# Two-layer gated cross-attention block: another way to turn the attention probabilities of layer 1

## What is computed

```python
def _L1_xattn_ref(X, encoder_out, Wq, bq, Wkv, bkv, Wo, bo):
    Q = (X @ Wq.T + bq).reshape(b, lq, h, d)
    KV = (encoder_out @ Wkv.T + bkv).reshape(b, lk, h, 2 * d)
    K, V = (KV[..., :d], KV[..., d:])
    scores = jnp.einsum('bqhd,bkhd->bhqk', Q, K) / SCALE
    weights = jax.nn.softmax(scores, axis=-1)
    attn = jnp.einsum('bhqk,bkhd->bqhd', weights, V).reshape(b, lq, h * d)
    return attn @ Wo.T + bo
```

## Time and profile before

| | us |
|---|---|
| median of 3 runs | 1371.87 (1369.77 to 1372.11) |
| the profiled execution, its own time | 1371.72 |
| its span in the profile | 1370.0 |
| PE, DVE, ACT, Pool busy | 1223.5, 1026.2, 769.0, 395.0 |
| mean granted clock of PE | 0.972 of 2.4 GHz |

### The profile page before, as it was taken

One profiled execution on the slowest core, in us unless ns is written; L12 is line 12 of the kernel. 1 busy time (PEld: TensorE's weight loads), 2 busy tenths in 40 slices (PEclk: granted clock), 3 DMA queues, 4 the chain that ended last, 5 costly groups with the idle time before them and its releaser, 6 DMA issues.

```text
span 1370.0 us, 27816 instructions
## 1 busy us (share of the span) xinstructions
PE 1223.5 (89%) x10408; PEld 760.9 (56%) x10408; DVE 1026.2 (75%) x1662; ACT 769.0 (56%) x1013; POOL 395.0 (29%) x248
## 2 busy tenths in 40 slices
PE   0869899999999996788799999999999999999974
PEld 0335565566566566334356666656666666666642
DVE  6656666666666646877888888888888888888877
ACT  0525455555555555455666666666666666666642
POOL 6357666666566415332000000000000000000000
PEclk9979999999999997999999999999999999999996
DMA  5223244234333420010011110011110011110000
GB/s 151 76 78 79 80 114 113 77 101 110 96 90 104 116 58 18 0 46 0 8 38 46 46 44 22 25 45 45 45 45 20 26 44 45 45 45 23 1 0 14
DMA packets 29717, 74.66 MB, mean 54 GB/s; under 512 B 6384, under 2 KB 14960, under 8 KB 29664
## 3 DMA queue, kind: packets, MB, share of 16 engines
q1 hardware_dynamic: 23408, 70.78, 17.7%
q10 hardware_dynamic: 6256, 3.16, 0.9%
HBM read 42.30 MB, written 0.46 MB: 31 GB/s over the span
## 4 chain that ended last, share of the span: by engine, by line
PE 69%; DVE 13%; issue 8%; ACT 7%; ACTq 3%; POOL 0%; DVEq 0%
PE bank L826 13%; PE bank L808 13%; PE bank L768 8%; PE bank L684 7%; PE bank L708 5%; PE bank L712 5%; PE bank L725 4%; DVE bank_max L1497 3%; ACTq L416 2%; DVE region L1639 2%; PE bank L849 2%; ACT region L1141 2%; PE bank L797 2%; DVE e_row L1458 2%; PE bank L1053 2%
## 5 line engine op out<-in xcount | busy, mean ns | idle before, releaser
L1458 DVE CUSTOM_DVE_ANT_0 e_row<-bank,region 112x1500 f32<-112x1500 f32 x128 | 220.1, 1720 | 129.4 <-PE bank L684 128.4
L1176 ACT CAST region<-bank 125x768 f16<-125x768 f32 x224 | 178.7, 798 | 206.2 <-PE bank L768 206.2
L1141 ACT ACTIVATE region<-bank 125x896 f32<-125x896 f32 x192 | 176.0, 917 | 210.0 <-PE bank L712 209.9
L808 PE MATMUL bank<-region 128*128 128x500 f16 x1008 | 234.6, 378 | 14.7 <-ACT e_row L1167 13.3
L1516 DVE TENSOR_TENSOR region<-bank,region 125x768 f16<-125x768 f32 x224 | 209.7, 954 | 25.4 <-ACT region L1176 25.4
L1497 DVE TENSOR_REDUCE bank_max<-bank 128x1 f32<-128x500 f32 x336 | 208.8, 671 | 10.6 <-PE bank L808 10.6
L514 POOL TENSOR_TENSOR region<-c_in,region 125x1536 f16<-125x1536 f32 x16 | 49.7, 3108 | 560.8 <-ACT region L1191 560.8
L768 PEld LDWEIGHTS bank<-ident,e_row 128*125 128x125 f32 x1344 | 175.5, 188 | 31.2 <-DVE region L1516 5.5
L768 PE MATMUL bank<-ident,e_row 128*125 128x128 f32 x1344 | 179.5, 273 | 3.3 <-DVE region L1516 2.6
L1167 ACT ACTIVATE e_row<-bank,neg_max 128x1500 f32<-128x1500 f32 x112 | 169.7, 1515 | 20.2 <-DVE neg_max L1501 20.0
L808 PEld LDWEIGHTS bank<-region 128*128 (+1 forms) x1008 | 93.3, 98 | 115.6 <-issue 11.4
(11 more groups left out here) (212 smaller groups left out, 1471.0 us busy)
## 6 DMA issues: line engine op xcount, KB each, us to landing
c_in<-in_ctx SPq DMA_DIRECT2D x32, 750.0 KB
region<-region SPq DMA_DIRECT2D x64, 192.0 KB, 2.7
region<-in_mask_Bx1xSxS_if SPq DMA_DIRECT2D x32, 328.1 KB
region<-region SPq DMA_DIRECT2D x64, 96.0 KB, 2.5
region<-region SPq DMA_DIRECT2D x8, 750.0 KB
...
```

What stands on the lines that cost most here:

```text
L808: last = pe.matmul(bank[:, k, 0:4 * KP], q1[:, ql, b, 128 * t:128 * (t + 1)], c_t1[par][:, cl, 4 * k:4 * k + 4, 0:KP], start=(ql == 0 and ...
L1141: act.activation(p0[:, 2 * i:2 * i + 2, :], ring0("s", h, i)[0:KP, :, 0:HALF_ROWS], ACT.Exp, scale=SCALE0)\
L1176: act.copy(p_high1[grp][:, UC * u:UC * (u + 1), 128 * at:128 * (at + 1)], pair_chunks(unit_no(1, par, ("turn", t, u)), 128)).then_inc(sem( ...
L1458: dve.tensor_tensor_reduce(out=masked.rearrange("p (a k) -> p a k", a=3), in0=bank[0:R0, 0:3, 0:4 * KP], in1=mask_bias[par][:].rearrange(" ...
```

## The change

- The scores use banks 0 to 2 and 3 to 5 in turn (`score_banks1`), so those of tile t+1 wait for the exponential of t-1, and not of t. The maximum is one instruction over the three banks.
- The rows are not scaled in place. DVE makes 1/sum with the factor 2^14 folded in (`dve_inv1`), Pool multiplies and casts to the high 16-bit halves (`pool_high1`), and DVE computes e x 1/sum - high in one instruction to the low halves (`dve_low1`), all before turning, into `halves1` (two buffers).
- The low halves are turned by a DMA transpose from SP, tile by tile (`sync_turn1`). The high halves are turned by PE with twelve 16-bit transposes in two sixes through one bank (`pe_turn1`, bank 6) and copied out by ACT.
- The split context is turned by one DMA transpose (`sync_turn_context1`), not by PE and ACT. Pool makes its low half after the high half of tile 2.
- The products start one tile later, and the order on PE, ACT, DVE, Pool and SP is written anew. Some semaphores are renamed or merged.

```diff
-        c_split1 = carve([128, KC, 2, E], F16)
-        c_keep1 = [carve([128, KC, 2, E], F16)[0:KP],
...
-        p_high1 = [carve([KP, KC, 128 * (b - a)], F16) for a, b in GROUPS1]
-        p_low1 = [carve([KP, KC, 128 * (b - a)], F16) for a, b in GROUPS1]
+        p1 = [carve([128, 2, KC, 128 * (b - a)], F16) for a, b in GROUPS1]
...
+        halves1 = [t.bitcast(F16).rearrange("p (n c k) -> p n c k", n=2, c=KC)
+                   for t in (u_flat[:, tern_words:tern_words + KC * 128], wg_sb[:].rearrange("p n j h -> p (n j h)"))]
...
+        T_BANK = 6
+        def score_banks1(par, t):
+            first = 3 * ((t + par) % 2)
+            return bank[:, first:first + 3, 0:4 * KP]
...
+        def turned1(b, par, t):
+            return sem(f"turned1_{(t + par) % 2}"), 56 * (b - par) + 16 * ((T1 * par + t) // 2 + 1)
+        def sync_turn1(sp, b, par, t):
+            grp = 0 if t < GROUPS1[1][0] else 1
+            first = GROUPS1[grp][0]
+            if t == first:
+                wait_apart(sp, "sp", (sem("pv_done1"), 2 * (b - 1) + grp + 1))
+            wait_apart(sp, "sp", (sem("low_done1"), b * T1 + t + 1))
+            sp.dma_start_transpose(p1[grp][:, 1, :, 128 * (t - first):128 * (t - first + 1)],
+                                   halves1[(t + par) % 2][:, 1].rearrange("p c k -> p (c k)"))\
+                .then_inc(turned1(b, par, t)[0], 16)
+        def sync_turn_context1(sp, b, par):
+            wait_apart(sp, "sp", (sem("split_done1"), b + 1))
+            wait_apart(sp, "sp", (sem("scores1"), (b - 1) * T1))
+            sp.dma_start_transpose(c_t1[par].rearrange("p n c k -> p (n c) k"), c_split1.rearrange("p n c e -> p (n c e)"))\
+                .then_inc(sem("c_turned1"), 16)
...
                 if not last:
                     sync_load_context(sp, 1, b + 1, 1 - par)
-                    sync_keep(sp, b + 1, 1 - par)
+                for t in range(T1):
+                    sync_turn1(sp, b, par, t)
+                    if t == 2 and not last:
+                        sync_turn_context1(sp, b + 1, 1 - par)
+                    if t == GROUPS1[1][0] and not last:
...
+        def pool_high1(pool, b, par, t):
+            wait_apart(pool, "pool", (sem("inv_done1"), 2 * (b * T1 + t) + 2), (sem("turned_high1"), 2 * (b * T1 + t - 1)))
+            pool.tensor_scalar(halves1[(t + par) % 2][:, 0, :, 0:KP], e_row[(t + par) % 2][:].rearrange("p (c k) -> p c k", c=KC),
+                               row_inv[:, t:t + 1], None, ALU.mult).then_inc(sem("high_done1"), 1)
...
-            batches(pool, lambda b, par, first, last: None if last else pool_context1(pool, b + 1, 1 - par))
+            def layer1(b, par, first, last):
+                for t in range(T1):
+                    pool_high1(pool, b, par, t)
+                    if t == 2 and not last:
+                        pool_context1(pool, b + 1, 1 - par)
+            batches(pool, layer1)
...
+        def turned_half1():
+            return bank[:, T_BANK, :].bitcast(F16)[:, 0:UC * 128]
+        def pe_turn1(pe, b, par, t, u, after_proj=False):
+            if u == 0:
+                pe.wait_ge(sem("high_done1"), b * T1 + t + 1)
+            wait(pe, sem("high_copied1"), 2 * (b * T1 + t) + u)
+            if after_proj:
+                pe.wait_ge(sem("block_done1"), b)
+            if isinstance(b, int) and (b, t, u) == (B - 1, 1, 0):
+                pe.wait_ge(sem("residual"), 2 * TT + EARLY)
+            for c in range(UC):
+                last = pe.transpose(turned_half1()[:, 128 * c:128 * (c + 1)], halves1[(t + par) % 2][:, 0, UC * u + c, :],
+                                    ident16[:])
+            last.then_inc(sem("turned_high1"), 1)
...
         def pe_scores1(pe, b, par, t):
             if t == 0:
-                for n in range(2):
-                    pe.wait_ge(sem(f"ct_done1_{n}"), b + 1)
-            wait(pe, sem("exp_done1"), b * T1 + t)
+                if isinstance(b, int) and b == 0:
+                    for n in range(2):
+                        pe.wait_ge(sem(f"ct_done1_{n}"), 1)
+                else:
+                    pe.wait_ge(sem("c_turned1"), b * 16)
+            wait(pe, sem("exp_done1"), b * T1 + t - 1)
             for k in range(3):
                 for ql, cl in ((0, 0), (0, 1), (1, 0)):
-                    last = pe.matmul(bank[:, k, 0:4 * KP], q1[:, ql, b, 128 * t:128 * (t + 1)],
+                    last = pe.matmul(score_banks1(par, t)[:, k, :], q1[:, ql, b, 128 * t:128 * (t + 1)],
                                      c_t1[par][:, cl, 4 * k:4 * k + 4, 0:KP],
                                      start=(ql == 0 and cl == 0), stop=(ql == 1))
-                last.then_inc(sem("scores1"), 1)
+            last.then_inc(sem("scores1"), 1)
...
-                pe.wait_ge(sem("kept1"), (b + 1) * 16)
+                for t in (z - 2, z - 1):
+                    pe.wait_ge(*turned1(b, par, t))
+                pe.wait_ge(sem("high_copied1"), 2 * (b * T1 + z))
+                wait(pe, sem("u_done1"), 2 * b + grp)
+                if grp == 0:
+                    pe.wait_ge(sem("kept1"), (b + 1) * 16)
             for c in range(first, end):
-                for cl, p in ((0, p_high1), (0, p_low1), (1, p_high1)):
-                    last = pe.matmul(bank[:, U_BANK, 0:cols], c_keep1[par][:, c, cl, :], p[grp][:, c, :],
-                                     start=(c == 0 and cl == 0 and p is p_high1),
-                                     stop=(c == KC - 1 and cl == 1))
+                for cl, pl in ((0, 0), (0, 1), (1, 0)):
+                    last = pe.matmul(bank[:, U_BANK, 0:cols], c_keep1[par][:, cl, c, :], p1[grp][0:KP, pl, c, :],
+                                     start=(c == 0 and cl + pl == 0), stop=(c == KC - 1 and cl == 1))
...
-                    pe_turn(pe, 1, b, par, t, (0,))
-                    if t == 0:
-                        pe_turn(pe, 1, b, par, t, (1,))
-                    if t < 3 and not first:
-                        pe_pv1(pe, b - 1, 1 - par, 1, 4 * t, 4 * t + 4)
-                    if t >= 4:
-                        pe_pv1(pe, b, par, 0, 4 * (t - 4), 4 * (t - 3))
-                    if t > 0:
-                        pe_turn(pe, 1, b, par, t, (1,))
-                    if t == PROJ_AT and par == 0 and not first:
+                    turn = (b, par, t - 1) if t > 0 else (b - 1, 1 - par, T1 - 1)
+                    has_turn = not (first and t == 0)
+                    proj = t == T1 - 1 and par == 0 and not first
+                    if t >= 5:
+                        product = (b, par, 0, 4 * (t - 5))
+                    elif t == 0:
+                        product = (b - 1, 1 - par, 0, 8)
+                    else:
+                        product = (b - 1, 1 - par, 1, 4 * (t - 2))
+                    has_product = t != 1 and (t >= 5 or not first)
+                    if proj:
+                        pe.wait_ge(sem("high_copied1"), 2 * (b * T1 + t - 1))
                         pe_proj1(pe, b)
-                    if t in PREP_AT[1] and not last:
-                        pe_prep(pe, 1, b + 1, 1 - par, (PREP_AT[1].index(t),))
-                    if t == PREP_AT[1][0] and last:
-                        wait_pair(pe, 1, b, par, PREP_0)
+                    elif has_turn:
+                        pe_turn1(pe, *turn, 0)
+                    if has_product:
+                        pe_pv1(pe, *product, product[3] + 2)
+                    if has_turn:
+                        pe_turn1(pe, *turn, 0 if proj else 1, proj)
+                    if has_product:
+                        pe_pv1(pe, *product[:3], product[3] + 2, product[3] + 4)
+                    if proj:
+                        pe_turn1(pe, *turn, 1)
+                    if last and t == 1:
+                        pe.wait_ge(sem("u_done1"), 2 * b - 1)
+                        pe.wait_ge(sem("high_copied1"), 2 * (b * T1 + 1))
                         pe_block_turn(pe, B - 2, range(EARLY), early_turned, "block_done1")
...
-            pe_pv1(pe, B - 1, 1, 1, 0, 7)
+            pe_turn1(pe, B - 1, 1, T1 - 1, 0)
+            pe_pv1(pe, B - 1, 1, 0, 8, KC)
+            pe_turn1(pe, B - 1, 1, T1 - 1, 1)
...
-            pe_pv1(pe, B - 1, 1, 1, 7, KC)
+            pe_pv1(pe, B - 1, 1, 1, 0, KC)
...
         def act_exp1(act, b, par, t):
             act.wait_ge(sem("max_done1"), b * T1 + t + 1)
-            wait(act, sem("turned1"), (b * T1 + t - 1) * 2)
-            act.activation(e_row[(t + par) % 2][:], bank[:, 0:3, 0:4 * KP], ACT.Exp, bias=neg_max[:, t:t + 1],
-                           accum_out=row_sum[:, t:t + 1]).then_inc(sem("exp_done1"), 1)
+            wait(act, sem("low_done1"), b * T1 + t - 1)
+            act.activation(e_row[(t + par) % 2][:].rearrange("p (a k) -> p a k", a=3), score_banks1(par, t), ACT.Exp,
...
+                wait(act, sem("pv_done1"), 2 * (b - 1) + grp + 1)
+            act.copy(p1[grp][:, 0, UC * u:UC * (u + 1), 128 * at:128 * (at + 1)],
```

(62 more changed lines are left out.)

165 lines of the change are left out of this document (57 added, 108 removed).

## The result

The changed kernel takes 1488.05 us (median of 4 runs, 1485.80 to 1488.91) where the kernel before takes 1371.61 beside it: 1.085 times as long (95% interval 1.083 to 1.087), 116 us more. The profiled execution is 1487.50, its span 1485.7. The forecast was 1460.

The account below looks back on a forecast made before the run. The bound was to move from PE to a chain of inverse, Pool's cast and low: 112 x 6.22 = 697 us plus 43 for collisions, 740 against 656; with the end +88, so 1460. The range for 8 in 10 was 1300 to 1550.

Parts of the forecast that it names:

- the ring: Layer-1 attention: inverse, Pool's cast and DVE's low follow one another in every tile, 6.22 us a tile, 43.6 a batch.
- Rival 1: Layer 1: Pool casts at the plain cast's rate, 1.43 us, and PE bounds again, 1306 us; chance 0.22.
- The other links: Each layer-1 tile, beside Pool's cast: inverse 0.35 us, release of Pool 0.18, release of DVE with low 1.71.
- The collision: Once a batch DVE's low of tile 2 and Pool's context subtraction take turns: 2.9 us in 15 batches, 43 us.
- the cost of the clock: Layer 1: PE idles longer, which may lower its granted clock; taken as zero, up to 2 us a batch (30 us).
- The end: After layer 1's last tile: 21 products no longer run in PE's free time before the up-projection, 3.4 us, +4 taken.
- The DMAs: Layer 1: SP's transposing transfers stay hidden, each with at least a tile to spare; 384 KB costs some 3.4 us.
- rival 3: Layer 1: the DMA transposes bound above some 4 us each; at 5, 54 us a batch, about 1585; chance 0.10.
- the fourth case: Layer 1: low of tile 2 and Pool's subtraction don't collide, 1 us instead of 2.9 a batch, 1430; no separate chance.

Follow-up runs that it names:

- the first experiment: The changed kernel with Pool's high cast as a plain 32 to 16 bit copy, without the factor: 1304.54 us, 0.951 times the kernel before.
- the half-and-half kernel: The changed kernel with the high cast of tiles 0, 2, 4 and 6 on ACT and of the rest on DVE: 1344.59 us, 0.981 times the kernel before.

## Why the prediction held, and by how much its steps were off

The direction and the mechanism held, the size was 28 us short of 116. Step by step:

- **The bound moves from PE to the ring.** Right. The cast was forecast at 3.98 from the 2304-column rows and took 4.07. Rival 1 (1.43) is the plain cast's rate, and the first experiment shows that it is right for the plain cast (1.441 us) and wrong for the multiplication. What it would have given was forecast at 1306, and the kernel with the plain cast takes 1304.5. The Trainium skill, GPSIMD Engine Reference, Engine selection, calls one-input work on GpSimd "roughly line-rate" and two-input work about half as fast. The cast agrees with it; the multiplication by a factor doesn't, and the same product as a two-input operation is the faster of the two (2.69 against 4.07).
- **The other links.** Inverse 0.34 (0.35 forecast), release of Pool 0.23 (0.18), release of DVE 0.04 in one buffer's tiles and 0.13 in the other's, then 1.70 of low (1.71 together). With the cast at 4.07 this is 6.38 and 6.47, 6.42 on average against 6.22. Over all 94 ordinary steps from cast to cast the mean is 6.43, since the step from one batch to the next takes 6.57. So the links are 112 x 0.21 = 24 us of the 28. What was mis-sized is three small terms of the same sign: 0.09 the cast, 0.05 Pool's release, 0.07 low with its release. A ring has no slack, so every tenth in it counts 112 times, where errors in the busy time of an engine off the chain count nothing.
- **The collision.** Forecast 2.9 us, 43 in all; 2.8 in all 15 batches of the timeline, 41.5 in all, and 2.6 by the experiment that cuts it. Right, in mechanism and size.
- **PE.** Forecast 35.6 busy a batch, measured 38.0, since it runs at a granted clock of 0.89 and 0.93 in these batches where it had 1.00 before. I had put the cost of the clock at zero, and inside the batches it stays there: the ring's links add up to the batch without it, and with the subtraction cut the clock is 0.97 (from 1000 to 1100 us) while the ordinary steps stay at 6.37 and 6.46. With the cast on DVE the clock is 1.00 again and PE busy 34.7. The lower clock goes with PE's idle time. At the end of the layer it does cost something, as the next point shows.
- **The end.** Layer 1's last low ends at 1436.35 and the up-projection's first matmul starts 15.5 us later, at 1451.82. The forecast was +4 there, for 21 of the 36 products; from last low to the end of the span it is 49.4 against 41.3 before, +8.0. The step missed another item in the same queue. (The section on the kernel before says that Pool does nothing but the subtraction in layer 1; it also makes the root of the early normalisation there, at 1311.12, with an idle queue.) The changed kernel's timeline of Pool shows it:

```profile
1430.47 4.07 POOL L502 TENSOR_SCALAR wg_sb<-e_row,row_inv 128x1500 f16<-128x1500 f32 x1 [2.30 <-PE bank L786]
1434.51 0.24 POOL L495 TENSOR_SCALAR rstd<-mean_var 128x6 f32<-128x6 f32 x1
1434.83 2.73 POOL L497 TENSOR_TENSOR rstd<-rstd,half_neg 128x6 f32<-128x6 f32 x1
```

The normalisation on DVE:

```profile
1437.60 1.63 DVE L1452 TENSOR_SCALAR x_norm<-x_tok,mean_var,rstd 128x128 f32<-128x128 f32 x6 [1.24 <-POOL rstd L497]
```

And PE up to the up-projection:

```profile
1443.95 0.79 PE L1124 MATMUL bank<-ident_b,region 128*128 128x128 bf16 x6 [2.98 <-DVE region L1753]
1444.53 7.45 PE L826 MATMUL bank<-region,g_w 125*128 125x384 f16 x36
1451.82 1.03 PE L1099 MATMUL bank<-u_w,region 128*128 128x512 bf16 x4
```

  The reciprocal root of this normalisation is Pool's too, and stands behind the last cast; the normalisation waits 1.24 us for it and takes 1.63 itself, which in the kernel before had been done ahead of the last low; what follows it comes 3.0 us later behind that low. All 36 products now stand between the transposes and the up-projection, where the earlier trace rows has 21 of them in idle time: that is the 3.4 forecast. From the transposes to the up-projection the granted clock is 0.78, where it was 1.00, and this is the remaining 1.7.
- **The whole account.** The last low ends 107.7 us later than before (1436.35 against 1328.69), where 84 was forecast. Of the difference, 24 is the tile, less 1.5 for the collision. Another 3.0 is in two steps of the last batch, which take 7.93 and 7.92 us: DVE's work on the tokens (the residual at 1401.30, the statistics at 1415.60) stands between low and the inverse, so it is on the ring, a term that the forecast did not have. And 1.8 goes off, since the same stretch took 657.8 us before and not the 656 of sixteen average batches. With 8.0 behind the last low that makes 115.7.
- **The DMAs** hide, as forecast; rival 3 is out at one transpose a tile and only begins to show at two.
- **No collision** (the fourth case) would be 1449, not 1430, since the ring is longer than forecast.

What remains open: why a multiplication by a factor takes Pool so much longer than the product of two tensors, and why the granted clock of the half-and-half kernel is 0.96.
